# L1_ffn, L3_ffn and L2_ffn: projection, norm, transposes and router by halves of 128 tokens

## The reference

```python
# L1_ffn (L3_ffn alike: rmsnorm, softmax router, top 2 of 8, one shared expert)
x = x + attention(layer_norm(x, ln1_w), c_attn_w, c_proj_w)    # y @ c_proj_w.T at its end
x_ln = layer_norm(x, ln2_w)
logits = x_ln @ w_g.T                                          # 256 x 8
top_vals, top_idx = jax.lax.top_k(logits, 2)
probs = softmax(masked top_vals)
slot = position of the token among those of its expert; kept if slot < 64
h = gelu(einsum('ecd,edh->ech', dispatched, c_fc))             # 8 experts, 768 -> 1536
out = einsum('ech,ehd->ecd', h, c_proj_e)
x = x + einsum('tec,ecd->td', cb, out)

# L2_gnn, then L2_ffn on the normalised sum
out = segment_sum(a[:, :, None] * oj, dst) + b                 # second RGAT convolution, one head
x = x + out
probs = softmax(xf @ switch_w + switch_b)                      # top 1 of 8, capacity 40
h = gelu(einsum('ecd,edf->ecf', buf, w1) + b1)
o = einsum('ecf,efd->ecd', h, w2) + b2
```

## Time and profile before

| | us |
|---|---|
| median of 3 runs | 1833.15 (1831.13 to 1835.19) |
| the profiled execution | 1833.63 |
| its span, first to last instruction | 1831.8 |
| PE busy | 1733.0 (95% of the span) |
| DVE busy, ACT busy | 623.2 (34%), 444.4 (24%) |
| mean granted PE clock | 0.985 of full |

### The profile page before, as it was taken

How to read it: one execution, slowest core, us unless ns; L and a number is a source line. 1 busy time by engine, 2 the same in 40 slices (tenths; PEclk the granted TensorE clock), 3 DMA queues, 4 the chain that set the end, 5 groups by cost and what they waited for, 6 DMA issues and landing times.

```text
span 1831.8 us, 27529 instructions
## 1 busy us (share of the span) xinstructions
PE 1733.0 (95%) x12224; PEld 1040.4 (57%) x12224; DVE 623.2 (34%) x1177; ACT 444.4 (24%) x816; POOL 26.8 (1%) x35
## 2 busy tenths in 40 slices
PE   7999999999999999799999988887999999999998
PEld 4675445754476555577654433334675645768664
DVE  4415994049962211543210000002412422133231
ACT  0014883047831110433110000003411010131110
POOL 0000000000000000000000000000001000000000
PEclk9999999999999999899999999999999899999999
DMA  9205986149747877304579999999362164301661
GB/s 379 109 31 171 210 260 243 52 118 218 242 159 282 328 302 303 114 1 155 207 310 387 427 429 429 427 428 428 130 251 103 68 244 193 132 27 52 259 240 64
DMA packets 80750, 408.28 MB, mean 223 GB/s; under 512 B 9768, under 2 KB 50241, under 8 KB 58993
## 3 DMA queue, kind: packets, MB, share of 16 engines
q1 hardware_dynamic: 76112, 402.41, 58.1%
q10 hardware_dynamic: 4512, 4.03, 0.7%
HBM read 400.85 MB, written 5.51 MB: 222 GB/s over the span
## 4 chain that ended last, share of the span: by engine, by line
PE 80%; DMA 13%; DVE 4%; issue 1%; ACT 1%; SPq 0%; POOL 0%; DVEq 0%; ACTq 0%
PE banks L114 78%; DMA weight_ring<-in_L_ffn_c_fc_dram 8%; PE banks L117 2%; DMA weight_ring<-in_L_ffn_c_proj_e_dram 2%; DMA weight_ring<-in_L_gnn_W_in_dram 2%; DVE weight_ring L120 1%; DMA gate_queries<-in_L_gnn_query_rep_dram 1%; DMA node_parts<-gate_node_parts 1%; DVE stat L266 1%; DMA gate_rows<-node_parts 0%; DVE xn_tok L125 0%; DMA ident<-in_c_ident_dram 0%; SPq L154 0%; DVE xT L137 0%; ACT weight_ring L148 0%
## 5 line engine op out<-in xcount | busy, mean ns | idle before, releaser
L114 PE MATMUL banks<-weight_ring,xT 128*128 128x384 f32 x864 | 293.2, 491 | 1.5 <-DVE rgat_xr L137 1.5
L120 DVE TENSOR_TENSOR weight_ring<-weight_ring,gate_queries 128x1024 f32<-128x1024 f32 x192 | 222.7, 1221 | 18.9 <-ACT weight_ring L148 11.3
L114 PEld LDWEIGHTS banks<-weight_ring,xT 128*128 128x128 f32 x864 | 162.6, 191 | 109.0 <-issue 8.7
L148 ACT ACTIVATE weight_ring<-banks 128x1024 f32<-128x1024 f32 x192 | 191.0, 1024 | 44.0 <-PE banks L114 40.8
L114 PE MATMUL banks<-xT,weight_ring 128*128 128x256 f32 x792 | 178.2, 379 | 3.2 <-ACT x_tok L151 3.2
L114 PEld LDWEIGHTS banks<-xT,weight_ring 128*128 128x128 f32 x792 | 149.8, 190 | 27.4 <-issue 3.6
L114 PE MATMUL banks<-weight_ring,r_xd 128*32 128x384 f32 (+1 forms) x2304 | 142.7, 406 | 0.0
L114 PE MATMUL banks<-weight_ring,moe_xdT 128*64 128x384 f32 x720 | 122.0, 489 | 21.4 <-DMA weight_ring<-in_L_ffn_c_fc_dram 20.4
L114 PEld LDWEIGHTS banks<-weight_ring,r_xd 128*32 128x32 f32 x2304 | 76.7, 110 | 63.2 <-issue 54.9
L114 PE MATMUL banks<-gate_rows,selrow 96*128 96x512 bf16 x384 | 107.4, 381 | 2.9 <-ACT weight_ring L148 1.8
L114 PE MATMUL banks<-weight_ring,selrow 128*32 128x256 f32 x1536 | 102.0, 385 | 2.9 <-DVE weight_ring L120 2.7
(11 more groups left out here) (370 smaller groups left out, 1842.7 us busy)
## 6 DMA issues: line engine op xcount, KB each, us to landing
weight_ring<-in_L_ffn_c_fc_dram SPq DMA_DIRECT2D x30, 2304.0 KB, 23.1
weight_ring<-in_L_ffn_c_proj_e_dram SPq DMA_DIRECT2D x21, 2304.0 KB, 28.3
gate_queries<-in_L_gnn_query_rep_dram SPq DMA_DIRECT2D x48, 512.0 KB, 4.6
weight_slot_heads<-in_L_ffn_c_proj_e_dram SPq DMA_DIRECT2D x9, 2304.0 KB, 28.8
weight_ring<-in_L_ffn_w_gate_dram SPq DMA_DIRECT2D x8, 2304.0 KB, 9.8
weight_ring<-in_L_ffn_w_up_dram SPq DMA_DIRECT2D x8, 2304.0 KB, 8.9
weight_ring<-in_L_ffn_w_down_dram SPq DMA_DIRECT2D x8, 2304.0 KB, 9.6
weight_ring<-in_L_ffn_w_dram SPq DMA_DIRECT2D x16, 1152.0 KB, 7.6
```

Of the source, the lines that this page charges most:

```text
L114: return self.e.matmul(out, lhsT, rhs, start=start, stop=stop)
L120: return self.e.tensor_tensor(out, a, b, op)
L148: return self.e.activation(out, a, f, **kw)
```

## The change

`project_tok_pe` is replaced by `project_chunk_pe`, which does one chunk (12 products). It counts `projected` after chunk 0, and `unit_free` after chunk 1. `norm_dve` is cut into `variance_dve` and `rows_dve`, for one chunk each. Two new helpers put these together for L1_ffn and L3_ffn: on PE `project_and_logits_pe`, on DVE `norm_and_turn_dve`. On DVE, chunk 0 is normalised and copied while PE projects chunk 1; its transposes stand on PE before the last four products of chunk 1. The 8 and 9 idle products go. The residual products are cut into pairs and stand between the logits; in L1_ffn the last pair stands behind `slots_pe`. The logits go to bank 5. In L1_ffn `S` is built in two parts, experts 0 and 1 first, the first dispatch waits for that part alone, two idle products follow it, and the first expert waits for ACT's half of the dispatched tokens only at its fourth k.

In L2 each chunk is scaled, normalised and copied in one go (`rgat`'s end on DVE), the transposes of chunk 0 stand before the last three products of chunk 1's `weigh`, the ten idle products behind `weigh` go and seven stand between the logits and the transposes of chunk 1, and ACT's six DMAs move behind its exponentials. A semaphore of `overflow_dve_flag` gets another name, without an effect on the order.

The diff, cut to its core:

```diff
-        def project_tok_pe(pe, key, st, first=True):
+        def project_chunk_pe(pe, key, st, c, steps):
+
             w = w3(unit(key), DC, D)
             pe.wait_ge(*loaded(key))
-            for k in range(DC):
-                for c in range(TC):
-                    for h in range(2):
-                        t = pe.mm(PS[:, 2 * c + h, 0:HALF], st[:, k, c * P:(c + 1) * P],
-                                  w[:, k, h * HALF:(h + 1) * HALF], first and k == 0, k == DC - 1)
-            t.then_inc(*mark("unit_free", key))
+            for k in steps:
+                for h in range(2):
+                    t = pe.mm(PS[:, 2 * c + h, 0:HALF], st[:, k, c * P:(c + 1) * P],
+                              w[:, k, h * HALF:(h + 1) * HALF], False, k == DC - 1)
+            if k == DC - 1:
+                t.then_inc(*(mark("unit_free", key) if c else mark("projected", key)))
...
+                variance_dve(v, key, c, src, eps, eps_first, center)
             for c in range(TC):
-                mean, rstd = moments[:, c, 0:1], stat[:, 28 + c:29 + c]
-                d2, s2 = dst[:, 2 * c:2 * c + 2, :], src[:, 2 * c:2 * c + 2, :]
...
+        def variance_dve(v, key, c, src, eps, eps_first=None, center=True):
...
+        def rows_dve(v, key, c, dst, src, center=True):
...
+        def project_and_logits_pe(pe, key, unit_key, y, router, ready):
+
+            rows = key + "_2"
+            residual_pe(pe, y, True)
+            for f in range(DC):
+                pe.wait_ge(*at("yT", (key, f)))
+            project_chunk_pe(pe, unit_key, xT, 0, range(DC))
+            project_chunk_pe(pe, unit_key, xT, 1, range(4))
+            tok_to_T_pe(pe, rows, rows, (0,))
+            project_chunk_pe(pe, unit_key, xT, 1, range(4, DC))
+            pe.wait_ge(*ready)
+            wait_T(pe, rows, 0)
+            small_logits_pe(pe, key, xT, router, NEXP, None, 5, (0,))
+            pe.wait_ge(*at("kept", (key + "_y", 0)))
+            residual_pe(pe, x_tok, True, (0,))
+            tok_to_T_pe(pe, rows, rows, (1,))
+            residual_pe(pe, y, False, (0,))
+            wait_T(pe, rows, 1)
+            small_logits_pe(pe, key, xT, router, NEXP, None, 5, (1,))
+            pe.wait_ge(*at("kept", (key + "_y", 1)))
+            residual_pe(pe, x_tok, True, (1,))
+
+        def norm_and_turn_dve(v, key, unit_key, weight, eps, center=True):
+
+            rows = key + "_2"
+            for c in range(TC):
+                v.wait_ge(*(at("unit_free", unit_key) if c else at("projected", unit_key)))
+                variance_dve(v, rows, c, acc_tok, eps, None, center)
+                rows_dve(v, rows, c, as_tok(xn_tok[:]), acc_tok, center)
+                tok_to_T_dve(v, rows, weight, (c,))
...
-            v.tt(S3, bc(iota_slot[:, 1:SLOT + 1].unsqueeze(1), sh), bc(slot.rearrange("p c e -> p (c e)").unsqueeze(2), sh),
-                 ALU.is_equal).then_inc(*mark("S", key))
+            S4 = S[:].rearrange("p c (e s) -> p c e s", s=SLOT)
+            for part, own in (((key, "first"), slice(0, 2)), (key, slice(2, NEXP))):
+                n = [P, TC, own.stop - own.start, SLOT]
+                v.tt(S4[:, :, own, :], bc(iota_slot[:, 1:SLOT + 1].unsqueeze(1).unsqueeze(1), n),
+                     bc(slot[:, :, own].unsqueeze(3), n), ALU.is_equal).then_inc(*mark("S", part))
...
-            residual_pe(pe, y_tok, True)
-            for f in range(DC):
-                pe.wait_ge(*at("yT", ("L1_ffn", f)))
-            project_tok_pe(pe, "c_proj", xT, False)
-            idle_products_pe(pe, 8)
-            tok_to_T_pe(pe, "L1_ffn_2", "L1_ffn_2")
-            wait_T(pe, "L1_ffn_2")
-            pe.wait_ge(*ready)
-            small_logits_pe(pe, "L1_ffn", xT, wg, NEXP)
-            pe.wait_ge(*at("kept", ("L1_ffn_y", 1)))
-            residual_pe(pe, x_tok, True)
-            residual_pe(pe, y_tok, False)
+            project_and_logits_pe(pe, "L1_ffn", "c_proj", y_tok, wg, ready)
             slots_pe(pe, "L1_ffn", msc[1])
-            pe.wait_ge(*at("S", "L1_ffn"))
+            residual_pe(pe, y_tok, False, (1,))
+            pe.wait_ge(*at("S", ("L1_ffn", "first")))
             first_dispatch_pe(pe, "L1_ffn", mS)
-            wait_xd_of(pe, "L1_ffn", "first", "first")
+            idle_products_pe(pe, 2, 5)
+            pe.wait_ge(*at("xd_dve", ("L1_ffn", "first")))
...
+                            if n == 0 and k == DC // 2:
+                                pe.wait_ge(*at("xd_act", ("L1_ffn", "first")))
...
+                        if n == 0:
+                            pe.wait_ge(*at("S", "L1_ffn"))
...
+                            if l == 1 and c == 1 and n0 and j == NSRC // 2:
+                                tok_to_T_pe(pe, "L2_ffn", "L2_ffn", (0,))
...
-            v.then(t)
+                v.then(t)
+                variance_dve(v, "L2_ffn", c, as_tok(x_tok[:]), 1e-5)
+                rows_dve(v, "L2_ffn", c, as_tok(xn_tok[:]), as_tok(x_tok[:]))
+                tok_to_T_dve(v, "L2_ffn", None, (c,))
...
-            idle_products_pe(pe, 10)
-            tok_to_T_pe(pe, "L2_ffn", "L2_ffn")
-            wait_T(pe, "L2_ffn")
             pe.wait_ge(*ready)
-            small_logits_pe(pe, "L2_ffn", xT, sw, NEXP, swb[0:1, :])
-            idle_products_pe(pe, 3, 5)
+            wait_T(pe, "L2_ffn", 0)
+            small_logits_pe(pe, "L2_ffn", xT, sw, NEXP, swb[0:1, :], 5, (0,))
+            idle_products_pe(pe, 5)
+            tok_to_T_pe(pe, "L2_ffn", "L2_ffn", (1,))
+            idle_products_pe(pe, 2, 6)
+            wait_T(pe, "L2_ffn", 1)
+            small_logits_pe(pe, "L2_ffn", xT, sw, NEXP, swb[0:1, :], 5, (1,))
+            idle_products_pe(pe, 3, 4)
...
-            idle_products_pe(pe, 10, 5)
+            idle_products_pe(pe, 10, 4)
...
-            a.wait_ge(*at("variance", ("L2_ffn", 1)))
-            smalls_dma(a, "L3_gnn")
-            bias_parts_act(a)
             tok_to_T_act(a, "L2_ffn")
             a.wait_ge(*at("logits", "L2_ffn"))
             for c in range(TC):
                 t = a.act(wsc[1][:, c, :], wsc[0][:, c, :], ACT.Exp, bias=stat[:, 42 + c:43 + c],
                           accum=stat[:, 44 + c:45 + c])
             t.then_inc(*mark("logits_exp", "L2_ffn"))
+            bias_parts_act(a)
+            smalls_dma(a, "L3_gnn")
...
-            norm_dve(v, "L2_ffn", as_tok(xn_tok[:]), as_tok(x_tok[:]), 1e-5)
-            tok_to_T_dve(v, "L2_ffn")
...
-            residual_pe(pe, y3, True)
-            for f in range(DC):
-                pe.wait_ge(*at("yT", ("L3_ffn", f)))
-            project_tok_pe(pe, "L3o", xT, False)
-            idle_products_pe(pe, 9)
-            tok_to_T_pe(pe, "L3_ffn_2", "L3_ffn_2")
-            wait_T(pe, "L3_ffn_2")
-            pe.wait_ge(*ready)
-            small_logits_pe(pe, "L3_ffn", xT, gw, NEXP)
-            pe.wait_ge(*at("kept", ("L3_ffn_y", 1)))
-            residual_pe(pe, x_tok, True)
-            residual_pe(pe, y3, False)
+            project_and_logits_pe(pe, "L3_ffn", "L3o", y3, gw, ready)
+            residual_pe(pe, y3, False, (1,))
...
-            norm_dve(v, "L3_ffn_2", as_tok(xn_tok[:]), acc_tok, 1e-6, center=False,
-                     ready=lambda c: at("unit_free", "L3o"))
-            tok_to_T_dve(v, "L3_ffn_2", nw[:, 1, :])
+            norm_and_turn_dve(v, "L3_ffn", "L3o", nw[:, 1, :], 1e-6, False)
```

More of the change, by code:

```diff
@@ L286, in norm_pool @@
+        def rows_dve(v, key, c, dst, src, center=True):
+            mean, rstd = moments[:, c, 0:1], stat[:, 28 + c:29 + c]
+            d2, s2 = dst[:, 2 * c:2 * c + 2, :], src[:, 2 * c:2 * c + 2, :]
+            v.wait_ge(*at("rstd", (key, c)))
+            if center:
+                t = v.ts(d2, s2, mean, ALU.subtract, rstd, ALU.mult)
+            else:
+                t = v.ts(d2, s2, rstd, ALU.mult)
+            t.then_inc(*mark("rows", (key, c)))
         def norm_pool(g, key):
@@ L1642, in overflow_dve_flag @@
             s = B["stage"]
-            v.wait_ge(*at("worst_ps", s))
+            v.wait_ge(*at("slots_ps", (s, "worst")))
             v.then(v.red(stat[0:1, 53:54], PS[0:1, 4, 0:P], ALU.max))
@@ L3204, in L2_ffn_dve @@
             m, pmax, route, rank = (stat[:, i:i + 2] for i in (40, 44, 46, 48))
-            v.then(v.cp(logits, logits_of(4, NEXP)))
+            v.then(v.cp(logits, logits_of(5, NEXP)))
             v.then(v.red(m, logits, ALU.max))
```

74 lines of the change are left out of this document (34 added, 40 removed).

## The result

| us | before | after |
|---|---|---|
| median of the comparison, 5 runs each | 1833.15 (1828.05 to 1837.1) | 1814.99 (1809.16 to 1816.72) |
| profiled execution | 1833.63 | 1809.26 |
| its span | 1831.8 | 1807.4 |
| PE busy | 1733.0 | 1711.3 |

The ratio is 0.9888, 95% interval 0.9867 to 0.991: 18.2 us faster by the medians. The forecast was 1814.0, range 1810.5 to 1820.5. The profiled execution of after is one of the two fastest of its five, 5.7 us under their median. By the two timelines 22.4 us of them lie in the three places (10.1, 7.9 and 4.5), 1.5 lie ahead of L1_ffn's projection, where the change does nothing, and 0.6 in the stream of weights behind L1_ffn's first expert.

The account below looks back on a forecast made before the run. PE was taken to bound the kernel, with 80% of the chain. L1_ffn 8.3, L2 7.5 and L3_ffn 3.7 sum to 19.5 us off 1833.6, giving 1814.1, stated as 1814.0; range 1810.5 to 1820.5.

Parts of the forecast that it names:

- Bound and order of the work: Whole kernel: PE holds 80% of the chain, so time is won where PE waits or does work nobody needs.
- L1_ffn, 8.3 us: L1_ffn: slots 7.1 us earlier and experts starting between 912.2 and 913.3 instead of 921.0, taken as 8.3 us.
- the bounds 7.7 and 8.8: L1_ffn: lower and upper gain at the experts' start, by the side on which the clock falls.
- A low clock at the dispatch: Changed profile: the clock low at the dispatch was listed among the signs that would make the forecast wrong.
- L2, 7.5 us: L2: logits 6.3 us earlier, first comparison 8.0 earlier at full clock or 6.0 at the lower; 7.5 us taken.
- The move of ACT's DMAs: Start of L2_ffn: six DMA issues occupy ACT for 4.0 us, about 1.5 us of it on the path.
- L3_ffn, 3.7 us: L3_ffn: slots at 1662.2 instead of 1666.25, 4.05 us earlier; gain 2.35 to 4.05, taken as 3.7 us.
- The clock behind the mask's wait: L3_ffn, shared expert's products: if the clock drops there for 3.4 us at half speed, 1.7 us are given back.
- rival (a): L1_ffn's expert stage: transfers take back its 8.3 us, 11.2 remain, total 1822.4 us; chance 7%.
- (b): All three places: normalising a half takes up to 4.8 us, longer than its cover; total 1818.7 us; chance 5%.
- (c): All three places: without the idle products the clock falls, making the kernel 5.5 us slower, 1839 us; chance 3%.
- (d): The steps move but something unseen takes their place, up to half the gain, about 1824 us; chance 3%.

Follow-up runs that it names:

- l2_only: The kernel before with the change in L2 alone: median 1826.14 us, ratio 0.9963 to before.
- l3_only: The kernel before with the change in L3_ffn alone: median 1830.56 us, ratio 0.9988, not told from no change.
- l1_only: The kernel before with the change in L1_ffn alone: median 1826.53 us, ratio 0.9961 to before.
- filled: The changed kernel with L3_ffn's shared-expert gate product ahead of the slots and L1_ffn's two idle products dropped: median 1814.29 us, ratio 0.9895 to before.
- act_moved_only: The kernel before with only ACT's six DMA issues moved behind the exponentials: median 1832.07 us, ratio 0.999, not told from no change.
- act_back: The changed kernel with ACT's six DMA issues back ahead of its copies into xT in L2_ffn: median 1826.07 us, ratio 0.9967 to before.
- after_no_idle: The changed kernel without the idle products around its new code in L1_ffn and L2_ffn: median 1818.09 us, ratio 0.9923 to before.
- hold_l2: The changed kernel with eight more idle products in waits at the start of L2_gnn: median 1812.11 us, ratio 0.9885 to before.

## Why the prediction was right, step by step

**Bound and order of the work.** Right. The logits end 23.0 and 23.2 us behind the projection's start in L1_ffn and L3_ffn (23.5 said). Every step inside the three places came as placed; nothing unseen took its position.

**L1_ffn, 8.3 us.** 10.1 in the profiled pair, 6.8 against l2_only and l3_only (38.4), 6.9 by the median of l1_only. Right in the middle of these. The waits were sized well: 0.66 (0.4 said) and 1.36 (1.35), one half's normalisation 3.2 (3.15). The dispatch was sized too dear: 2.84 at the full clock, where 3.5 was built from the transposes' records; in three other kernels with this code 4.07 to 4.20, at a lower clock. The 0.9 us of idle products were to cover VectorE's copy and cover nothing (filled). The new code takes 31.68 us in two profiles and 33.3 in four with the same code of L1_ffn, the old one 41.8 or 38.4. So the gain lies anywhere from 5.1 to 10.1, by the pair of profiles taken, and the bounds 7.7 and 8.8 were too narrow: I varied the clock in the new code alone. A low clock at the dispatch was named as a sign against the forecast; in the other profiles it came, and cost 1.6 us of the gain, not all of it.

**L2, 7.5 us.** 7.9 in the pair, 6.6 against 38.09, 7.3 alone. The 6.6 is 4.9 if the stretch from the dispatch to L3_ffn is taken in, which took 169.7 us in l1_only and l3_only and 171.4 in after; whether the new code has a part in that isn't shown. Logits 24.0 (24.2 said), comparison 7.9 earlier (8.0 at the full clock). One half's normalisation took the 2.8 said, though its reason was off: rows from SBUF take 0.68 us where those from PSUM take 1.02, two thirds and not half. The move of ACT's DMAs was right as a row (1.6 measured in the kernel before). The Trainium skill, DMA: Bandwidth & Descriptors, Issuing engines are not separate DMA queues, calls the time to initiate a DMA "usually small relative to the DMA itself". For the two transfers whose landing the trace of before shows it agrees: 0.36 and 0.45 us of issue against 2.8 and 3.7 to landing. But the sentence compares with the transfer, and here the time counts on the issuing engine, whose next copy is on the path: six issues took 4.0 us of ACT in the earlier trace rows. The prediction's reading of it, that the move would be worth nothing, is refuted by the 1.6 us of act_moved_only. The prediction missed that the halves depend on the move.

**L3_ffn, 3.7 us.** 2.9 alone. The slots came 4.56 earlier (4.05 said; in a timeline a group's end reaches 0.15 over the next one's start, and I had added these durations up). The clock behind the mask's wait was the open term, 1.7 us: it fell in l3_only and act_back (7.11; the dispatch 2.8 earlier in l3_only) and did not in after (4.5 earlier), after_no_idle and hold_l2.

**Transfers, rival (a).** Out, by the 337 us above. **(b)** Out: 3.2 and 3.4 us. **(c)** Wrong in the form named. Taking the idle products out costs 6.3 us in the kernel before and makes L2_ffn of the changed one slower (33.46 for 31.49), so there they hold the clock; but the change keeps enough of them, and its pairs do their work in L1_ffn up to the slots. **(d)** Nothing seen.

**The sum.** 19.5 was said, 18.2 by the medians and 20.5 by the ratio (1833.15 times 0.0112). The three places give 16.2 us when both kernels have their best clock (6.8, 6.6, and 2.9 for L3's slots, 30.48 to 27.61), up to 22.4 when before alone has its low stretches, as in its profile (10.1, 7.9, 4.5), and less than 16.2 when the new code alone falls (L1_ffn 33.3 against 38.4). The prediction went by the profile of before, and how often the clock falls in it no single profile tells. The mechanism is shown step by step; that the forecast lies within 1.0 us of the median is in part luck, since the runs of the changed kernel alone spread over 7.6 us.

## What to carry to other kernels

Where PE waits for a row-wise normalisation, work by halves pays if full-width work of the same stage can stand between the narrow products; in L1_ffn that work also held the clock up to the slots, without an idle product. Before a step is cut in halves, look at each engine that serves it for what is queued ahead of the first half's copy: an order that cost 1.8 to 3.1 us at the dispatch before cost 10.9 afterwards. Idle products that are to cover a wait should be checked against the kernel without them: two of them here only took 0.85 us. A gain that is built from one profile should be bounded with the old code at the full clock too.
